# GpSimd normalises the second group of token tiles in both routers, in place of ScalarE

## The reference

```python
x = x + 0.5 * ffn(layernorm(x), gate_w, gate_b, w1, w2, w3, ws1, ws2, ws3)
x = x + attn(layernorm(x), W_qkv, b_qkv, W_out, b_out)
x = x + 0.5 * ffn(layernorm(x), gate_w, gate_b, w1, w2, w3, ws1, ws2, ws3)

def layernorm(x, eps=1e-05):
    m = jnp.mean(x, axis=-1, keepdims=True)
    v = jnp.var(x, axis=-1, keepdims=True)
    return (x - m) / jnp.sqrt(v + eps)

def ffn(x, ...):                                  # 64 experts, 6 per token, at most 64 tokens each
    scores = softmax(x @ gate_w.T)
    _, idx = top_k(scores + gate_b, 6)
    ...                                           # tokens sorted by expert, gathered into xb
    h = silu(xb @ w1) * (xb @ w3);  yb = h @ w2   # added back to their tokens, weighted
    z = silu(x @ ws1.T) * (x @ ws3.T) @ ws2.T     # the shared part, for all tokens
    return y + z
```

## Time and profile before

| | |
|---|---|
| median of 3 runs | 532.62 us (532.6, 532.62, 534.25) |
| the profiled execution | 532.9 us, of which 531.2 us are its span (first to last instruction) |
| busy: TensorE, VectorE, ScalarE, GpSimd | 356.6, 307.6, 207.8, 237.0 us |
| TensorE's mean granted clock | 0.793 of full speed |

### The profile page before, as it was taken

How to read it: one execution, slowest core, us unless ns; L and a number is a source line. 1 busy time by engine, 2 the same in 40 slices (tenths; PEclk the granted TensorE clock), 3 DMA queues, 4 the chain that set the end, 5 groups by cost and what they waited for, 6 DMA issues and landing times.

```text
span 531.2 us, 14693 instructions
## 1 busy us (share of the span) xinstructions
PE 356.6 (67%) x5808; PEld 263.3 (50%) x5812; DVE 307.6 (58%) x999; ACT 207.8 (39%) x543; POOL 237.0 (45%) x215
## 2 busy tenths in 40 slices
PE   0874589999960013598999999218848999998000
PEld 0851475666650012376788888118327667666000
DVE  6488363545430994454777775394985544545077
ACT  3983112322310067744677762169722232231000
POOL 7161747887872000403333333001537888887400
PEclk9987567999995556678999999657855699999555
DMA  8999961001015996000111111454200100100396
GB/s 272 369 268 341 318 185 15 5 11 14 5 6 218 407 401 239 2 2 2 40 40 40 40 40 49 109 218 139 61 8 8 12 11 6 17 5 6 108 426 257
DMA packets 49746, 62.64 MB, mean 118 GB/s; under 512 B 21701, under 2 KB 36248, under 8 KB 47183
## 3 DMA queue, kind: packets, MB, share of 16 engines
q1 hardware_dynamic: 37423, 60.51, 33.3%
q0 software_dynamic: 12288, 1.70, 3.2%
HBM read 39.53 MB, written 31.46 MB: 134 GB/s over the span
## 4 chain that ended last, share of the span: by engine, by line
PE 53%; DVE 23%; DMA 9%; ACT 6%; issue 5%; POOL 3%; SPq 1%; POOLq 0%; DVEq 0%; ACTq 0%
PE bank L769 6%; PE upper L864 5%; PE bank L705 5%; DVE X L957 5%; PE bank L718 5%; PE upper L705 4%; DMA Cb<-planes_d 4%; PE upper L778 3%; DVE Cb L1094 3%; DVE bn L962 3%; DVE Cb L1025 3%; POOL planes_d L452 3%; ACT Cb L560 2%; ACT A L508 2%; PE bank L880 2%
## 5 line engine op out<-in xcount | busy, mean ns | idle before, releaser
L452 POOL DMA_INDIRECT planes_d<-Bb,put_i x64 | 101.4, 1584 | 28.0 <-issue 14.8
L480 POOL TENSOR_TENSOR Bb<-Cb,chm 128x576 f32<-128x576 f32 x32 | 36.9, 1183 | 124.3 <-PE upper L909 69.6
L466 POOL DMA_INDIRECT A<-rows_d,tok_i x64 | 68.0, 1063 | 41.6 <-DVE put_i L1066 22.7
L672 PE MATMUL bank<-ident,A 128*128 128x128 f32 x96 | 21.3, 396 | 81.9 <-ACT A L508 65.1
L672 PEld LDWEIGHTS bank<-ident,A 128*128 128x128 f32 x96 | 17.0, 209 | 85.1 <-ACT A L508 52.3
L1106 DVE TENSOR_SCALAR Bb<-upper,A 64x128 f32<-64x128 f32 x128 | 44.4, 347 | 1.3
L1094 DVE TENSOR_TENSOR Cb<-Cb,upper 88x512 f32<-88x512 f32 x24 | 16.4, 683 | 44.8 <-ACT Cb L560 44.8
L769 PEld LDWEIGHTS bank<-ring,w1s 128*88 128x88 f32 x256 | 34.2, 191 | 8.0 <-issue 8.0
L433 POOL TENSOR_TENSOR Bb<-Eb,st 128x512 f32<-128x512 f32 x8 | 8.3, 1043 | 63.8 <-DVE st L1013 63.8
L560 ACT ACTIVATE Cb<-bank 88x512 f32<-88x512 f32 x24 | 14.2, 592 | 55.1 <-PE upper L705 55.1
L769 PE MATMUL bank<-ring,w3s 128*88 128x64 f32 x256 | 35.6, 270 | 0.0
(11 more groups left out here) (162 smaller groups left out, 804.7 us busy)
## 6 DMA issues: line engine op xcount, KB each, us to landing
planes_d<-zeros SPq DMA_DIRECT2D x8, 2048.0 KB, 15.9
rows_d<-A SPq DMA_DIRECT2D x8, 512.0 KB, 6.0
A<-planes_d SPq DMA_DIRECT2D x4, 1024.0 KB, 6.0
PL<-planes_d SPq DMA_DIRECT2D x4, 1024.0 KB, 10.0
Bb<-planes_d SPq DMA_DIRECT2D x4, 1024.0 KB, 13.7
Cb<-planes_d SPq DMA_DIRECT2D x4, 1024.0 KB, 18.0
w1s<-in_w1T SPq DMA_DIRECT2D x4, 704.0 KB
w3s<-in_w3T SPq DMA_DIRECT2D x4, 704.0 KB
```

Of the source, the lines that this page charges most:

```text
L452: pool.indirect_dma_start(out=planes_d[f], in_=Y[:, s, :], in_offset=None, out_offset=bass.IndirectOffsetOnAxis(ap=put_i[:, s:s + 1], axis=0),
L466: pool.indirect_dma_start(out=GAT[:, t % RING, :], out_offset=None, in_=rows_d, in_offset=bass.IndirectOffsetOnAxis(ap=tok_i[:, t:t + 1], ...
L480: pool.tensor_tensor(out=VX[:, :, :, c, :].rearrange("p q h f -> p (q h) f"), in0=VN.rearrange("p q h f -> p (q h) f"), in1=chm[:, c:c + 1 ...
L672: ins = pe.transpose(bank[g % 2][:, (i % 4) * P:(i % 4 + 1) * P], A[:, i, :], ident[:, :])
```

## The change

GpSimd executes the eight instructions that normalise the second group (tiles 8 to 15) in the norms n = 0 and n = 2; ScalarE leaves them out there. GpSimd uses `(x - mean) * scale` with both scalars per token, as VectorE's L987 does; ScalarE's form was `x * scale + (-mean * scale)`. The norm ahead of the attention (n = 1) stays as it was.

```diff
@@ gpsimd, ahead of the router's work
             for f in range(2):
 
+                pool.wait_ge(scale_ready, 2 * NG * f + 2)
+                for i in range(GI, 2 * GI):
+                    ins = pool.tensor_scalar(A[:, i, :], X[:, i, :], mv[:, i, 0:1], st[:, 4, i:i + 1], ALU.subtract, ALU.mult)
+                ins.then_inc(normed[1], 1)
                 pool.wait_ge(small_in, 16 * N_SMALL)
                 for g in range(NG):
                     pool.wait_ge(recip_ready, NG * f + g + 1)
@@ scalar, in norm(n)
-                    if 0 < j < NG:
+                    if 0 < j < NG and (n == 1 or j != 2):
                         normalise(j - 1)
```

## The result

The changed kernel takes 543.75 us (median of 4 runs, 542.07 to 546.02); the kernel before took 533.43 beside it. The ratio is 1.0177, with a 95% interval of 1.0132 to 1.0222: slower by 1.8%, some 9.4 us (the two medians differ by 10.3). The forecast was slower by 0.36%, with 8 chances in 10 for 532.6 to 536.9. Direction right, size wrong by a factor of five, and outside the range.

A forecast was written before the change was run, and what follows sets the result against it. The start of group 1's transposes in each router was taken to bound the kernel. +1.9 us (first router) and -0.05 (second) on the profiled 532.9 gave 534.8, or 534.5 for the median; 8 in 10 for 532.6 to 536.9.

The forecast's parts named there:

- What bounds the kernel: Both routers: the start of group 1's transposes is what matters; later work moves along, 12.20 us from there to VectorE.
- The price of one new instruction, 320 ns: GpSimd's normalisation: 320 ns from start to start, ends 250 and 460 ns; eight take 2.6 us against ScalarE's 3.1.
- the sign of being wrong: Profile after: the forecast is wrong if GpSimd's eight instructions take under 2 us or over 4.
- When GpSimd can start: First router: GpSimd is in the IOTA until 15.46, so it starts at 15.5, where ScalarE had started at 13.3.
- The turns with VectorE, first router: GpSimd and VectorE's L987 take turns: 4.9 instructions cost 0.15 us more each; GpSimd ends at 18.8, transposes start at 18.95.
- The wait for L952, second router: GpSimd waits for VectorE's 1.22 us addition, starting at 355.55 instead of 354.55; transposes 0.05 us earlier than before.
- Cover: GpSimd's next work (L433), SyncE's writes and the gathers come later and add nothing; TensorE's series keeps its length.
- GpSimd does not wait for VectorE: Rival, both routers: without waits between the engines, +1.2 and -0.95 us, 532.9; chance 0.09.
- the faster rival: Rival: ScalarE's shorter queue wins, needing GpSimd at 0.2 us an instruction or less and no L952 wait; 531.4; chance 0.04.
- The clock did not rise later: Rival, second router: TensorE's clock rises only after group 3's transposes and group 2's logits, 2.4 us more, 536.9; chance 0.05.
- The slow way: Rival: per-token scalars make each GpSimd instruction cost 1.04 us; first router +6.9, second +5.7, 545 us; chance 0.05.

The follow-up runs named there:

- the pricing run: Kernel before, with groups of eight GpSimd instructions in several forms added behind all other work; the form of the change took 785 ns each, 6.23 us for eight.
- add_first: Kernel with GpSimd normalising in the second router alone, with VectorE's addition for the last group moved ahead of the scales of group 1; one run, 543.14 us.
- r2_only: Changed kernel, but GpSimd normalises the second group in the second router alone, ScalarE in the first; 1.0061 of the kernel before.
- r1_only: Changed kernel, but GpSimd normalises the second group in the first router alone, ScalarE in the second; 1.012 of the kernel before.
- shared: Changed kernel, but GpSimd takes only the group's last four tiles (first router) or three (second), ScalarE the rest, IOTA behind GpSimd's tiles; 1.0003 of the kernel before.
- iota_later: Changed kernel with GpSimd's last constant, the IOTA, moved behind its eight instructions of the first router; 1.0096 of the kernel before.
- tt_form: Changed kernel with two broadcast TENSOR_TENSOR of 128x1024 (subtract, multiply) in place of the eight instructions with scalars, same place; 1.0037 of the kernel before.

## Why the prediction was wrong

*What bounds the kernel.* Right: the instant at which the transposes of group 1 may start carried nearly the whole effect (8.7 us at the two places, 9.4 by the ratio), and the series behind it kept its length (12.2 us from their start to the third maxima before and after).

*The price of one new instruction, 320 ns.* This is the step that failed. It is 785 ns alone and 0.83 us from start to start in place (6.62 / 8), and the eight took over 4 us, the sign of being wrong that I had named. I had bracketed it between AFFINE_SELECT and TENSOR_TENSOR, as if GpSimd's price went by how many large operands an instruction reads. It does not: the pricing run puts a tensor_scalar, even with one constant, above a tensor_tensor of the same size. My upper end of 460 ns was worked out from a form that turned out cheaper, with 200 ns fixed that no row shows, so it was no bound. With 6.23 us for eight in place of 2.6, the other terms as I wrote them, and the measured 0.4 for the meeting with VectorE, the sum is 15.5 + 6.23 + 0.15 + 0.4 = 22.3 for the first router (measured 22.16), and 355.55 + 6.23 + 0.15 = 361.9 for the second, 3.6 later than before (measured 3.6). Sum 8.8, against 9.4 by the ratio. The two runs that bear it out are the price alone and the cheaper form in the same place, which took the transposes' delay from 5.1 and 3.6 us to 2.4 and 1.1.

*When GpSimd can start.* Right: 15.44 for the forecast 15.5, and moving the IOTA gave 3.27 us back.

*The turns with VectorE, first router.* The mechanism was there, the size was not: GpSimd lost 0.39 us (6.62 against 6.23) where I had 0.73, and VectorE lost 0.43 (2.56 against 2.13). Only some 0.12 of GpSimd's loss fell beside VectorE's eight (16.62 to 19.18), in two instructions of 0.84. The rest is one instruction behind them, which ran beside VectorE's casts (L1001 to L1004, 19.10 to 19.93), of which I had thought nothing. What held it was not tested.

```profile
19.44 1.07 POOL L431 TENSOR_SCALAR A<-X,mv,st 128x128 f32<-128x128 f32 x1
```

*The wait for L952, second router.* Right, 1.0 us forecast; measured 0.92 (1707 - 785), and gone when the addition was moved.

The Trainium skill (SBUF — State Buffer, Who interferes with whom) states this rule, that a VectorE instruction with two SBUF inputs and a GpSimd instruction that reads SBUF exclude each other; trace and experiment agree with it.

*Cover.* Right for L433 and SyncE. The first gather's data landed 0.9 us later than the delay at its issue explains (7.90 us under way in place of 7.00). The same leg is 6.95 and 7.50 us in two runs whose first router is that of before (`add_first`, `r2_only`) and 8.28 in `r1_only`, so part of it is spread; what the rest is stays open.

*The rivals.* That GpSimd does not wait for VectorE is refuted by the 1707 ns. For the faster rival I gave 292 ns as the least of any GpSimd row with 128 columns; one AFFINE_SELECT took 284 ns, which moves nothing. The clock did not rise later in this trace (12.2 us from the transposes to the third maxima in both routers), but did in others. The slow way had 0.05. It was what happened, for a wider reason than the per-token scalars that I gave: they are 147 of the 785 ns. Its price of 1.04 us was too high, and 545 a little above the measured median. The line of the Trainium skill (GPSIMD Engine Reference, 4.1 Engine selection) that one-input work runs at roughly line rate on GpSimd seemed to support my low end. The pricing run does not bear it out for tensor_scalar: 3.4 ns a column with two per-token scalars, where TENSOR_TENSOR with two inputs has 1.9.

## What to carry to other kernels

Before moving work to another engine, price that very instruction form there, with its scalars and its operations; neighbours with as many operands are no bound, and a handful of instructions at the end of the program is enough to measure it. A queue that is free is not the same as a short path: here the receiving engine was idle for 30 us and the move still cost 3.6 us, because the consumer waits for the last tile and the new engine needs 6.6 us for what took 3.1. What started the consumer earlier than before was handing over only as many tiles as end together with the old engine's part, with the consumer of the first half not waiting for them; how much of that reaches the whole time stayed at the edge of what was measured.

## What the runs showed of the hardware

- GpSimd's IOTA of 128x4096, which reads no tile, held VectorE's tensor_scalar from SBUF to SBUF back: eight took 4.87 and 6.69 us beside it in place of 2.13 (`shared`, `iota_later`). A single one of them made up most of the loss, 3.28 and 4.26 us in place of 0.34, and ended 0.1 us behind the IOTA. In the kernel before, the same IOTA ran beside VectorE's statistics (L962, one input), and eight of these took 1.64 us as always. The Trainium skill (SBUF — State Buffer, Who interferes with whom) names tensor_scalar among the VectorE instructions that can use both port pairs, one of which they share with GpSimd, and says that in such a mode it and a GpSimd instruction exclude each other for a whole instruction, while one with a single SBUF input outside these modes does not contend; these runs agree.
- In that contest the loss goes by the length of the other's instruction: beside GpSimd instructions of 0.79 us VectorE's eight lost 0.43 us in all, beside one of 1.9 us 1.58 (`tt_form`), and beside the IOTA of 3.87 us 2.74 and, with tensor_scalars ahead of it, 4.56.
- TensorE's granted clock fell from 1.00 to 0.50 (2.4 to 1.2 GHz) while it was idle for 3.67 us in the middle of a router (`shared`), and eight transposes went from 1.11 to 1.94 us. In the traces of the change, of `shared` and of `add_first` it was 0.57 in the mean over 8 us of the attention while TensorE was busy throughout; what lowered it there, no run shows.
